# A gated cross-attention block on one core: the tiles of one batch's feed-forward part interleaved with the units of the next

## What is computed

```python
def act_quant(x):      # one scale per token
    scale = 127.0 / clip(max(abs(x), axis=-1), 1e-05)
    return clip(round(x * scale), -128, 127) / scale
def weight_quant(w):   # ternary
    scale = 1.0 / clip(mean(abs(w)), 1e-05)
    return clip(round(w * scale), -1, 1) / scale
h = bit_linear(layernorm(x), w1)          # 512 -> 2048 hidden units
h = silu(depthwise_conv1d(h, conv_w, 3 taps over the tokens) + conv_b)
x = x + tanh(g_ffn) * bit_linear(h, w2)   # 2048 -> 512, h quantized per token
```

## Time and profile before

| | |
|---|---|
| median of 3 runs | 1693.51 us (1690.1 to 1697.37) |
| the profiled execution | 1691.95 us, its span 1690.1 us |
| feed-forward part in the span | 1284 to 1690 us |
| PE, DVE, ACT, POOL busy in it | 339, 313, 328, 157 of 406 us |
| instructions | 23527 |

### The profile page before, as it was taken

The page is one execution under the profiler, slowest core; times in us unless marked ns, Lnnn a source line. Parts: engine busy times, 40 slices in busy tenths (PEclk is TensorE's granted clock), DMA queues, the critical chain, the costliest instruction groups (busy, mean ns, idle before and its releaser), DMA issues. The chain is left out here.

```text
span 1690.1 us, 23527 instructions
## 1 busy us (share of the span) xinstructions
PE 1592.1 (94%) x8370; PEld 1001.8 (59%) x8370; DVE 1130.5 (67%) x2237; ACT 856.5 (51%) x974; POOL 725.2 (43%) x314
## 2 busy tenths in 40 slices
PE   6899999999999999999999999999999798897968
PEld 5788878888886644555445544554455454454534
DVE  7777636444444767766776687667537959969493
ACT  3233323333331254433665265526657978879676
POOL 1231000000000099974987588857944605336160
PEclk9999999999999999999999999999999999998989
DMA  7787656555534352222333133213244020110202
GB/s 259 268 273 256 213 184 232 212 187 192 192 141 172 120 206 76 76 88 83 119 126 113 64 138 126 101 54 110 89 150 150 1 82 13 47 54 7 94 1 82
DMA packets 116408, 217.67 MB, mean 129 GB/s; under 512 B 10056, under 2 KB 35656, under 8 KB 116304
## 3 DMA queue, kind: packets, MB, share of 16 engines
q1 hardware_dynamic: 116304, 216.31, 36.6%
HBM read 133.16 MB, written 83.12 MB: 128 GB/s over the span
## 5 line engine op out<-in xcount | busy, mean ns | idle before, releaser
L812 POOL TENSOR_TENSOR acc<-acc,pr 128x1024 f32<-128x1024 f32 x188 | 448.7, 2387 | 92.7 <-ACT pr L842 71.8
L842 ACT ACTIVATE pr<-ps,mcol 128x1024 f32<-128x1024 f32 x256 | 275.1, 1114 | 317.0 <-PE ps L1639 316.6
L1140 DVE CUSTOM_DVE_ANT_0 junk<-ps,mbias 128x512 bf16<-128x512 f32 x512 | 332.6, 688 | 105.3 <-PE ps L1612 105.1
L1651 PE MATMUL ps<-pr,vv 128*64 128x512 f32 x1024 | 261.0, 608 | 0.0
L819 POOL TENSOR_TENSOR h_first<-h_first,last_tap 128x1023 f32<-128x1023 f32 x43 | 105.3, 2450 | 174.8 <-DVE h_first L1489 144.2
L1612 PE MATMUL ps<-kh,qh 64*128 64x512 f32 x512 | 150.2, 471 | 5.2 <-DVE nmv L1140 4.4
L1612 PEld LDWEIGHTS ps<-kh,qh 64*128 64x128 f32 x512 | 68.4, 184 | 139.3 <-issue 56.3
L793 POOL MEMSET nmt<- 128x128 f32 x1 | 0.2, 205 | 344.0 <-DVE chl L1375 344.0
L1745 PE MATMUL ps<-xiT,w1q 128*128 128x512 bf16 x512 | 121.2, 380 | 2.7 <-DVE x2t L1518 2.7
L1902 PE MATMUL ps<-w2q,hq 128*128 128x512 bf16 x512 | 121.9, 392 | 2.0 <-ACT hq L1030 1.3
L812 POOL TENSOR_TENSOR acc<-pr 128x1024 f32<-128x1024 f32 x32 | 76.7, 2396 | 105.3 <-ACT pr L842 105.3
(11 more groups left out here) (181 smaller groups left out, 3141.9 us busy)
## 6 DMA issues: line engine op xcount, KB each, us to landing
craw<-in_ctxT SPq DMA_DIRECT2D x8, 2048.0 KB, 8.8
xa<-in_x SPq DMA_DIRECT2D x32, 256.0 KB, 3.8
wraw<-in_w1T SPq DMA_DIRECT2D x16, 512.0 KB, 5.9
wraw<-in_w2T SPq DMA_DIRECT2D x16, 512.0 KB, 6.8
q_split<-kqh SPq DMA_DIRECT2D x32, 256.0 KB, 2.0
q_split<-kql SPq DMA_DIRECT2D x32, 256.0 KB, 2.3
base<-lna SPq DMA_DIRECT2D x32, 256.0 KB, 4.0
k_split<-kqh SPq DMA_DIRECT2D x32, 256.0 KB, 2.0
```

Source lines behind the costliest of these rows:

```text
L812: nc.gpsimd.tensor_tensor(acc[:, blk % 2, :], first, pr[:, (8 * blk + j) % NP, :], ALU.add).then_inc(pool_acc, 1)
L842: act.activation(pr[:, u % NP, :], ps[:, 2 * (u % 2):2 * (u % 2) + 2, :].rearrange("p a t -> p (a t)"), ACT.Exp, bias=mcol[:, (u // 64) * ...
L1140: dve.tensor_tensor_reduce(out=(junk1 if n < LEAD and n % 2 else junk)[:, e, :], in0=ps[:, first_bank(n) + e, :], in1=mbias[:, b % 2, kk * ...
L1651: last = pe.matmul(ps[64 * e:64 * e + 64, 6 + blk % 2, :], vv[g % 2][:, j, 64 * e:64 * e + 64], pr[:, u % NP, e * CH:(e + 1) * CH], start= ...
```

## The change

`hT` is laid out in 2 x 8 x 8 blocks, by the unit's parity and its half number and by the token tile, and the last two change places from one batch to the next (`unit_cells`, `token_cells`). Units 2i and 2i+1 of the next batch so fill exactly the cells of token tile i of this batch. All lists then go by slots m = -1 to 31: slot m does tile m of the 32, prepares tiles m+1 and m+2, and works on units n = 2m+20 and n+1 of the 64 while there are any. Batch 0's sixteen units stay ahead of the slots, and the eight tiles of batch 3 come behind the last unit.

Within a slot, PE does `pe_first(n)`, half of `second`, `turn_units(n-2)`, half of `turn_h`, and the same again. PSUM: from unit 16 on units alternate between two pairs of banks (three before); bank 4 takes both halves of the turned tile, bank 5 the output. So `turn_h`, `hq` and the output have one bank each, where there were two pairs.

The rounding moves: ACT scales and adds the constant (`round_up`, one instruction of 128x2048, with per-token scale and a bias column), POOL takes it off (`take_off`, 128x2048 to bf16; halves of 1024 for the first tile of a batch), ACT copies the first half of `hq`, DVE the second (`second_half`). The norm of the last batch is split: statistics on DVE while the attention part ends (`last_stats`), normalization and integers on POOL (`last_norm`, slots 0 to 3; `last_integers`, slots 6 to 9; 32 instructions of 128x512), maxima on DVE (slots 1 to 4). SP loads `xn` ahead of the `x2` tiles. The square root of that norm moves on ACT ahead of the first Silu. The core of the diff:

```diff
-        hT = sb("hT", [P, NT, HID], F32)
+        hT = sb("hT", [P, 2, NT, NT, P], F32)
...
+        def pair_bank(n):
+            return 2 * (n % 3) if n < KH else 2 - 2 * (n % 2)
...
+        TURN_BANK, OUT_BANK = 4, 5
...
+        def unit_cells(n):
+            b, j = n // KH, n % KH
+            return hT[:, j % 2, :, j // 2, :] if b % 2 else hT[:, j % 2, j // 2, :, :]
...
+        LN_AT = {m: ("turn", B - 2, m) for m in range(NT // 2)} | {7: ("row", B - 1, 0), 8: ("row", B - 1, 1)} \
+            | {9 + u: ("turn", B - 1, u) for u in range(NT // 2)}
...
+            def take_off(m):
+                pool.wait_ge(act_d, D_ACT[f"r{m}"])
+                if m >= 2:
+                    pool.wait_ge(pe_ht, 2 * m - 2)
+                nc.gpsimd.tensor_scalar(int_cells(m), token_cells(m), MAGIC, None, ALU.subtract).then_inc(pool_sub, 1)
+
+            def take_off_halves(m):
+                for parity, name in enumerate((f"re{m}", f"r{m}")):
+                    pool.wait_ge(act_d, D_ACT[name])
+                    if m >= 2:
+                        pool.wait_ge(pe_ht, 2 * m - 2)
+                    nc.gpsimd.tensor_scalar(int_half(m, parity), token_half(m, parity), MAGIC, None, ALU.subtract).then_inc(pool_sub, 1)
+
+            def last_norm(i):
+                if i == 0:
+                    pool.wait_ge(dve_ln, LN_DVE["rstd"])
+                    pool.wait_ge(sp_xn_in, 16)
+                nc.gpsimd.tensor_scalar(xn[:, i, :], xn[:, i, :], mv2[:, i, 0:1], None, ALU.subtract).then_inc(pool_ln, 1)
+                pool.wait_ge(pool_ln, LN_POOL[f"off{i}"])
+                nc.gpsimd.tensor_scalar(xn[:, i, :], xn[:, i, :], rs2[:, 1, i:i + 1], None, ALU.mult).then_inc(pool_ln, 1)
+
+            def last_integers(i):
+                if i == 0:
+                    pool.wait_ge(act_sc, 1)
+                    pool.wait_ge(pe_xt, (B - 1) * (NT // 2))
+                    pool.wait_ge(dve_ln, LN_DVE[f"am{NT - 1}"])
+                nc.gpsimd.tensor_scalar(xn[:, i, :], xn[:, i, :], asc[:, i:i + 1], MAGIC, ALU.mult, ALU.add).then_inc(pool_ln, 1)
+                pool.wait_ge(pool_ln, LN_POOL[f"xr{i}"])
+                nc.gpsimd.tensor_scalar(xi[:, i, :], xn[:, i, :], MAGIC, None, ALU.subtract).then_inc(pool_ln, 1)
+
+            for n in range(KH + 1):
+                tap(n)
+            for m in range(-1, TILE_N):
+                last = m % NT == NT - 1 and m + 1 < TILE_N
+                if last:
+                    take_off_halves(m + 1)
+                if m == -1:
+                    tap(KH + 1)
+                if 2 * m + 20 < UNIT_N:
+                    tap(2 * m + 20)
+                if m + 2 < TILE_N and (m + 2) % NT:
+                    take_off(m + 2)
+                if 2 * m + 21 < UNIT_N:
+                    tap(2 * m + 21)
+                if 0 <= m < NT // 2:
+                    last_norm(2 * m)
+                    last_norm(2 * m + 1)
+                if 6 <= m < 6 + NT // 2:
+                    last_integers(2 * (m - 6))
+                    last_integers(2 * (m - 6) + 1)
...
+            def silu(n):
+                act.wait_ge(pe_ct, n + 1)
+                if n >= KH:
+                    act.wait_ge(pool_sub, SUBS[freed(n)])
+                act.activation(unit_cells(n), ps[:, 6:8, :].rearrange("p a (i t) -> p (a i) t", t=P), ACT.Silu).then_inc(act_d, 1)
+
+            def scale_of(m):
+                return hsc[:, m // NT % 2, m % NT:m % NT + 1]
+
+            def round_halves(m):
+                act.wait_ge(dve_d, D_DVE[f"hsc{m // NT}"])
+                for parity in range(2):
+                    act.activation(token_half(m, parity), token_half(m, parity), ACT.Identity, bias=magic,
+                                   scale=scale_of(m)).then_inc(act_d, 1)
+
+            def round_up(m):
+                act.wait_ge(dve_d, D_DVE[f"hsc{m // NT}"])
+                act.activation(token_cells(m), token_cells(m), ACT.Identity, bias=magic, scale=scale_of(m)).then_inc(act_d, 1)
+
+            def first_half(m):
+                act.wait_ge(pe_ht, 2 * m + 1)
+                if m >= 2:
+                    act.wait_ge(pe_o, m - 1)
+                act.activation(hq[:, m % 2, 0:KH // 2].rearrange("p j t -> p (j t)"), ps[:, TURN_BANK, :].bitcast(BF16), ACT.Copy).then_inc(act_d, 1)
...
+            for m in range(-1, TILE_N):
+                n = 2 * m + 20
+                last = m % NT == NT - 1 and m + 1 < TILE_N
+                if m - 1 in LN_AT:
+                    kind, b, u = LN_AT[m - 1]
+                    if kind == "row":
+                        act_ln_half_row(act, u)
+                    else:
+                        act_ln_turned(act, b, u)
+                if m == 6:
+                    act.wait_ge(dve_ln, LN_DVE["rec"])
+                    act.activation(asc[:], asc[:], ACT.Copy, scale=127.0).then_inc(act_sc, 1)
+                    act.activation(adq[:, B - 1, :], amax[:], ACT.Copy, scale=deq1).then_inc(act_sc, 1)
+                if last:
+                    round_halves(m + 1)
+                if n < UNIT_N:
+                    taps(n)
+                if n - 2 < UNIT_N:
+                    silu(n - 2)
+                if m == -1:
+                    act_ln_row(act, B - 2)
+                if last:
+                    round_up(m + 2)
+                if m + 1 < TILE_N:
+                    first_half(m + 1)
+                if not last and m + 2 < TILE_N and (m + 2) % NT:
+                    round_up(m + 2)
+                if n + 1 < UNIT_N:
+                    taps(n + 1)
+                if n - 1 < UNIT_N:
+                    silu(n - 1)
...
+            def last_stats(i):
+                dve.wait_ge(dve_free5, use5["y", B - 1, i] + 1)
+                dve.bn_stats(st2[:, i, :], bx[:, i, :]).then_inc(dve_ln, 1)
+                dve.wait_ge(dve_ln, LN_DVE[f"stat{i}"])
+                dve.bn_aggr(mv2[:, i, :], st2[:, i, :]).then_inc(dve_ln, 1)
...
+            def second_half(m):
+                dve.wait_ge(pe_ht, 2 * m + 2)
+                if m >= 2:
+                    dve.wait_ge(pe_o, m - 1)
+                dve.tensor_copy(hq[:, m % 2, KH // 2:KH].rearrange("p j t -> p (j t)"), ps[:, TURN_BANK, :].bitcast(BF16)).then_inc(dve_d, 1)
...
+            biggest(KH - 2)
+            first_tap(KH)
+            for m in range(-1, TILE_N):
+                n = 2 * m + 20
+                if m % NT == NT - 1 and m + 1 < TILE_N:
+                    biggest(n - 3)
+                    unit_scales((m + 1) // NT)
+                if m == -1:
+                    first_tap(n - 1)
+                    dve_diagonal(dve, B - 2)
+                if n < UNIT_N:
+                    dve_scaled(dve, n)
+                if m % NT != NT - 1 and n - 3 < UNIT_N:
+                    biggest(n - 3)
+                if n < UNIT_N:
+                    first_tap(n)
+                if n - 2 < UNIT_N:
+                    biggest(n - 2)
+                if n + 1 < UNIT_N:
+                    dve_scaled(dve, n + 1)
+                if m >= 0:
+                    add_out(m)
+                if m + 1 < TILE_N:
+                    second_half(m + 1)
+                if n + 1 < UNIT_N:
+                    first_tap(n + 1)
+                if 1 <= m < 1 + NT // 2:
+                    dve_last_max(dve, 2 * m - 2)
+                    dve_last_max(dve, 2 * m - 1)
+                if m == 1 + NT // 2:
+                    dve_last_scales(dve)
+                if m == 6:
+                    dve_diagonal(dve, B - 1)
...
+            if n >= 3:
+                back = n - 3 if n <= KH else n - 2
+                pe.wait_ge(dve_d, D_DVE[f"c{back}"])
+                pe.wait_ge(act_d, D_ACT[f"u{back}"])
...
+            for m in range(-1, TILE_N):
+                n = 2 * m + 20
+                if n < UNIT_N:
+                    pe_first(pe, n)
+                if m == -1:
+                    ln_row(pe, B - 2)
+                else:
+                    second(m, 0)
+                if n - 2 < UNIT_N:
+                    turn_units(n - 2)
+                if m + 1 < TILE_N and m % NT != NT - 1:
+                    turn_h(m + 1, 0)
+                if n + 1 < UNIT_N:
+                    pe_first(pe, n + 1)
+                if m >= 0:
+                    second(m, 1)
+                if m + 1 < TILE_N and m % NT == NT - 1:
+                    turn_h(m + 1, 0)
+                if n - 1 < UNIT_N:
+                    turn_units(n - 1)
+                if m + 1 < TILE_N:
+                    turn_h(m + 1, 1)
+                if m in LN_AT:
+                    kind, b, u = LN_AT[m]
+                    pe.wait_ge(dve_d, D_DVE[f"o{m}"])
+                    if kind == "row":
+                        ln_half_row(pe, u)
+                    else:
+                        ln_turn(pe, b, u)
...
```

More of the change, by code:

```diff
@@ L469, in flamingo_gated_block @@
[L469 to L484 removed]
+        LN_LAST, _ = counts(["row0", "row1"] + [f"xT{i}" for i in range(NT // 2)])
@@ new lines, in flamingo_gated_block, with ln_done @@
```

(67 more changed lines are left out.)

478 lines of the change are left out of this document (178 added, 300 removed).

## The result

The changed kernel takes 1738.89 us (median of 4 runs, 1733.35 to 1741.83), the kernel before 1694.3 in the same comparison: ratio 1.0261 (95% interval 1.0224 to 1.0298), 44.6 us slower. The forecast was 1678, at most 1700. The profiled execution took 1741.83 us, its span is 1739.6 (1690.1 before).

What follows compares the result with a forecast made beforehand. DVE bounds unit stages, PE tile stages; interleaved, hand-offs set slots of 10.6 to 10.65 us. 1363.0 + 234.3 + 6.7 + 9.6 = 1613.6; the 62.2 tail gives 1675.8, plus 1.85 outside 1677.7, called 1678; range 1664 to 1700.

Steps and rivals of the forecast that it cites:

- POOL's sum: POOL's work in a two-unit, one-tile slot: two additions of 2.37 and take_off at 2.4, 7.1 us.
- the tail's loop: Last tiles: turn half 0.6, copy 0.93, round 2.09, take_off 2.4, turn; 6.1 us per tile against 4.35 before.
- The new waits: Waits the change adds between engines in a slot, such as Silu's for take_off; single banks put at no cost there.
- POOL's subtraction goes at the rate of its addition: Rival: take_off takes 4.8 us, lengthening tail and norm slots; 36 us more, 1714 us; chance 0.10.
- Step 1: Start: last-batch statistics put off the first c from 1284.05 by 1.0 us; the reciprocal adds 0.2, g(17) waits 0.9.
- Step 2: First slot, m = -1: scales, taps and scaling, then units 18 and 19, put t(20) at 1363.0.
- Step 3: The 22 slots m = 0 to 21 at 10.65 us each from t(n) to t(n+2): 234.3 us.
- Step 4: Batch turns at m = 7 and 15: maximum, scales and rounding halves make t(n) 3.35 us late, 6.7 together.
- Step 5: Last batch's norm: DVE maxima 4.9, scales and diagonal 2.0, PE's turns delaying the second half of hq 2.7 us.
- Step 6: Tail from t(64) to the end: 15.6 us, then 6 tiles at 6.1, last addition at 59.0; 62.2 us.
- saves nothing per slot: Rival: late hand-offs keep a slot at 11.25 us, as long as its parts before; 13.2 more, 1691; chance 0.20.
- The rival with PE at half clock: Rival: PE drops to half clock in the tail, 9.7 us a tile; 21 more, 1699; chance 0.03.

Runs made afterwards that it cites:

- the probe: The kernel before with 21 single POOL instructions added, each waiting for the one ahead, to time their forms; its profiled execution took 1692.05 us.
- x2_two_ops_norm: The changed kernel with take_off and the norm's three one-operation POOL instructions written as two operations; 1679.48 us, 0.9931 of the kernel before.
- x7_norm_fast_only: The changed kernel with only the norm's POOL instructions in two operations, take_off staying one subtraction; 1726.98 us, 1.0206 of the kernel before.
- x4_scale_first: x2_two_ops_norm with DVE scaling unit n+2 ahead of the first tap of unit n+1; 1675.24 us, 0.9895 of the kernel before.

## Why the prediction was wrong, and where it was right

**The step that failed is the price of `take_off` in POOL's sum and in the tail's loop, 2.4 us where it took 5.37, and with it that of the norm's instructions on POOL, put at nothing where each took 1.5 to 1.6.** The sum took 2.4 us because a cast was the only one-input instruction of POOL in the trace of before. A cast, by the probe, has the fast rate (0.61 for 512); a lone subtraction has not (1.49). The fast and the slow form differ by a factor 2.8 at 2048 elements, and 5.37 lies even above the far bound of 4.8, which was POOL's two-input addition. Numbers in a neighbouring row priced the data streams and not the arithmetic. The sentence of the Trainium skill that was weighed, "GPSIMD Engine Reference", section 4.1, "roughly line-rate" for one input, holds here for one form and not for the other, and the estimate of 3.1 us from its section 3.1 fits neither 1.90 nor 5.37. The four norm instructions of a slot had no step in the sum at all for POOL; the rival priced them at 1.2 and they took 1.57. The new waits followed from this: Silu's for `take_off`, put at nothing, came to 20.9 us.

**The rival named it.** "POOL's subtraction goes at the rate of its addition" had the mechanism and both places: the tail's loop (8.5 forecast at 4.8, 9.2 to 9.6 measured at 5.37) and the slots with four norm instructions (14.4 us forecast, 16.4 measured). It gave 1714 and a chance of 0.10; with the measured prices its own formulas give a tail loop of 3.7 + 5.37 = 9.1 and slots of 16.4. Set against `x2_two_ops_norm` slot by slot, the slots behind the norm's four instructions cost 19.2 us (m = 2 to 5) where it gave 10, those with integers 11.4 (m = 7 and 9 to 11) where it gave 10. Of the 19.2, 15.3 are still there in `x7_norm_fast_only`, where the norm is in the form of `x2_two_ops_norm` and only `take_off` is slow. The range ended at 1700 because that case, at 0.10, was left out. By the profiles the loss splits so: t(62) is at 1640.55, so t(64) would be at 1651.2, less 4.49 is 1646.7, against 1613.6: 33.1 in the slots. From there to the end are 88.4 us against 62.2: 26.2 in the tail.

**With POOL's price put right, the sum comes out within 1 us, in part by luck.** Step by step:

- Step 1, start + 1.0: c of unit 0 moved from 1284.05 to 1289.48 - 4.49 = 1284.99. Right.
- Step 2, t(20) at 1363.0: 1363.8 after, 1362.2 in `x2_two_ops_norm` (each less the shift of its attention part). Right to 0.8.
- Step 3, 10.6 to 10.65 a slot, ACT's idle time ended by g: 10.68, and `x4_scale_first` shows that it is this loop. The parts are right too: rounding 2048 on ACT 2.11 (2.09), half of `hq` 1.03.
- The second half of `hq` on DVE was bounded at 1.2 by the rows. It takes 0.69 (next row, of `x2_two_ops_norm`). The prediction's estimate of 0.65 from the Trainium skill, "VectorE: DVE Perf Modes", "Why PSUM operands drop a tier", is near it; the trace agrees.

```profile
1616.47 0.69 DVE L1596 COPY hq<-ps 128x1024 bf16<-128x1024 bf16 x1 [0.50 <-PE ps L1958]
```

- Step 4, 3.35 a turn: too small. In `x2_two_ops_norm` the slots m = 6 and 7 together are 7.1 over 10.68 each, m = 14 and 15 5.1: 12.2 against 6.7.
- Step 5, the norm: the maxima cost 1.2 to 1.3 in each of four slots, 4.9 together, as forecast. The 2.7 for the late half of `hq` and most of the 2.0 did not come; 0.8 did.
- Steps 3 to 5 for `x2_two_ops_norm`: t(64) would be at 1602.70 + 10.68 = 1613.4; its attention part ended 1.55 earlier than before (1248.40), so 1614.9 against 1613.6.
- Step 6, the tail: 61.1 against 62.2, at 5.70 a tile. With 1.90 in place of 2.4 the loop of the prediction is 5.6 and its tail 15.6 + 6 x 5.6 + 10.0 = 59.2, so the tail was 1.9 too short, and the price of 2.4, too high for the fast form, hid it.

The whole: span 1674.5 + 1.55 = 1676.05 against the forecast 1675.8. The errors of steps 4 and 5 nearly cancel (+5.5 and -3.9), so that the agreement to 0.3 us is luck; the loop of a slot is not. With POOL in the fast form the interleaving saves 14 us in this execution, the fastest of its four, and 12.5 by the medians (1692.01 less 1679.48), against the 14 forecast. The changed kernel loses them and some 45 more to the form of 28 + 8 + 24 instructions.

The rival "saves nothing per slot" falls with the 10.68 where it had 11.25. The rival with PE at half clock explains little: after, 8 matmuls took 3.56 us (1682.67, behind a wait of PE for POOL of 3.90), and two of the tail's tiles were 9.58 apart instead of 9.17, 0.8 us together. The granted clock was 0.90 in the slots held by POOL (next row, 1390 to 1440; POOL busy 49.44 of 50), and is 1.00 in the same window of `x2_two_ops_norm`.

```profile
1390.00:1440.00 50.00, 36.24 (x210) 19.75 (x211) 29.98 (x31) 29.68 (x26) 49.44 (x23) 0.90 0.10 32
```

## What to carry to other kernels

Before work is moved to an engine, price the very instruction there, with its operation, not its neighbour with the same number of inputs. Where no row shows it, run a single one first, or let the range reach to the case in which it is slow; here that was a factor 2.2 over the price taken. And count the other instructions queued behind it. On POOL, try a lone operation as a pair of multiplication and addition (times 1, plus a constant) before giving the move up. And when a wait is taken out of a loop, ask in each kind of slot what is next: here 1.1 us a slot was real in five slots of 21.
